# SyncE's row reads in a five-layer graph network: byte offsets from lists, 32 registers a load, h_edge zeroed in quarters

## The chip, the core and the metric

The kernel runs on one core of a Trainium2 chip. The metric is the device time of one execution in microseconds; lower is better. The time before is the median of three runs.

## The reference

Five graph layers run one after the other on 12,500 nodes and 412,500 edges sorted by destination node, with 64 features a node. Each of the first four reads, for every edge, one row of a table of transformed source nodes, and adds the weighted rows up for each destination:

```python
def _rgat_conv(x, src, dst, etype, W, Q, K, b):          # layers 0 and 1 (CONV1, CONV2); 8 relations, 4 heads
    xw = jnp.einsum('ni,rio->rno', x, W)
    alpha = jax.nn.leaky_relu(qn[etype, dst] + kn[etype, src], 0.2)
    ex = jnp.exp(alpha - amax[dst])
    attn = ex / (denom[dst] + 1e-16)
    out_j = xw[etype, src].reshape(-1, H, hc // H)
    agg = jax.ops.segment_sum(attn[:, :, None] * out_j, dst, num_segments=n)
```

Layer 2 (GAT) is the same with one relation and one head; layer 3 (RGCN) sums `xw[etype, src] * edge_weight`; layer 4 (GINE) adds a message relu(h[src] + edge_attr) from every edge and runs a small network of two matrix products on the sum. What matters here is the read `xw[etype, src]` or `h[src]`: 412,672 rows (with padding) of 256 to 272 bytes in each of four layers.

## The kernel before, in words

Edges lie in 128 partitions of 3,224 edges each. A layer's edge pass goes over them in 52 chunks of 62 columns (`CH = 52`, `J = 62`), so a chunk is 128 x 62 edges. The loop body holds two chunks, `b` = 0 and 1, with a buffer `G[:, b]` each, and runs 26 times. I call two chunks a pair, and the edge pass of layer l pass l.

A chunk's rows come from two engines at once. GpSimd (POOL) issues one indirect DMA for each of the first 61 columns (`JP = J - 1`), each of 128 rows, through the helper `gather` (L652, called in the loop of L767 to L771). SyncE (SP) reads the last column, row by row. For each chunk it loads a list of 128 row numbers from DRAM into `row_list` (L607), waits until the buffer may be written (`idx_ready`, L609) and until the list is in (`list_in`, L611), loads 16 numbers at a time into registers (`sp.load`, L613, `RUN = 16`), copies them (`snap`, L614) and issues one small DMA for each row (L615): 128 DMAs a chunk. In pass 0 alone it also writes a 2 MB slice of zeros into `h_edge` after every chunk (L619), which layer 4 needs and GpSimd waits for at L721 (`big_zero`).

VectorE (DVE) waits for both sources of a chunk (`gathered` and `rows_in`, L1946 to L1948; in RGCN L1849 to L1851), then does the scores and the running sums (L1950 onwards) with ScalarE (ACT). In the middle of that work it copies the indices of the chunk two further on (`next_indices`, L1911) and raises `idx_ready`, which lets GpSimd and SyncE refill that buffer. ScalarE stores the sums (L870 to L879). When the last chunk's sums are stored, GpSimd reads the sums at the ends of the nodes (`gather_ends`, L652 with `fix_i` and then `end_i`), and the next layer's table is made.

Ahead of pass 0 lies a start of some 447 us. In it SyncE issues the input loads in order, among them two that pick one column out of every chunk (L522, L523: `src` and `edge_type_8` as `c p j` with j fixed, so that every element of 4 bytes stands alone), then the two stores of `dst_f` and `sub_last` (L528, L529). These two stores release GpSimd's first indirect reads, the search for the ends of the nodes, whose results the rest of the start needs. VectorE makes the relation-specific row numbers from the two lists at L1329, and SyncE writes both lists to DRAM (L531, L532).

## Time and profile before

| What | Value |
|---|---|
| Median device time of 3 runs | 36401.83 us (36386.37 to 36415.52) |
| Span of the profiled execution, first to last instruction | 22678.7 us |
| What the trace does not cover (median less span) | 13723.1 us |
| PE busy | 5315.0 us, 23% |
| DVE busy | 10606.0 us, 47% |
| ACT busy | 5421.1 us, 24% |
| POOL busy | 16413.3 us, 72% |
| POOL `region<-table,idx` (L652) | 12688 indirect DMAs, 944 ns each |
| SP `region<-table` (L615) | 26624 DMAs |

The page gives no total time for the profiled execution beside its span; the 13723.1 us between the span and the median are seen in no view. Engines work in parallel, so busy shares don't add up; a "releaser" is what ended an engine's idle time. SP's own instructions (register loads, register arithmetic, DMA issues) are not counted as busy, but they are listed with their durations as SPq.

### The profile page before, as it was taken

How to read it: one execution, taken by the hardware profiler on the slowest of the kernel's cores; microseconds unless marked ns; L12 is line 12 of the kernel's file. 1: busy time of each engine (PE TensorE's matmuls, PEld its weight loads, DVE VectorE, ACT ScalarE, POOL GpSimd, SP SyncE). 2: the span in 40 equal slices, each digit the busy share in tenths (PEclk: the TensorE clock that was granted, in tenths of full speed). 3: DMA queues.
4: the chain of work that ended last, by engine and by line, in shares of the span. 5: the costliest groups of instructions: out<-in, count | busy, mean ns of one | idle time of the engine just before them, and what ended most of it. 6: DMA issues, size and time to landing. Idle time of an engine off the chain costs nothing.

```text
span 22678.7 us, 201879 instructions
## 1 busy us (share of the span) xinstructions
PE 5315.0 (23%) x30665; PEld 3876.7 (17%) x30665; DVE 10606.0 (47%) x9480; ACT 5421.1 (24%) x4707; POOL 16413.3 (72%) x17069
## 2 busy tenths in 40 slices
PE   2000000020000001222222266666662222222201
PEld 1000000010000001222222255555552000000001
DVE  2444444324444443556566668888884111111167
ACT  1222222222222222111111132222221211121175
POOL 7777777677777776777777767777776777777733
PEclk9999999999999999666666655555555666666655
DMA  6333333332222222222222232222222222222164
GB/s 203 95 98 101 95 98 98 88 97 76 70 75 70 72 73 46 54 54 58 54 57 55 52 87 56 52 56 52 56 52 61 84 76 76 76 80 80 66 235 162
DMA packets 782414, 1839.84 MB, mean 81 GB/s; under 512 B 380834, under 2 KB 415306, under 8 KB 720302
## 3 DMA queue, kind: packets, MB, share of 16 engines
q0 software_dynamic: 544128, 569.36, 13.8%
q10 hardware_dynamic: 88736, 721.35, 8.1%
q1 hardware_dynamic: 148622, 541.43, 6.7%
q14 instruction: 915, 7.50, 0.1%
q8 instruction: 13, 0.21, 0.0%
HBM read 1007.43 MB, written 929.12 MB: 85 GB/s over the span
## 4 chain that ended last, share of the span: by engine, by line
POOL 55%; issue 24%; SPq 12%; DMA 3%; DVE 2%; PE 2%; ACT 1%; POOLq 0%; DVEq 0%; ACTq 0%
POOL region L652 41%; POOL by_src L742 12%; SPq L615 9%; SPq L613 3%; DMA region<-by_src 2%; DMA row_list<-row_lists 1%; POOL q_rel L713 1%; SPq L614 1%; PE ps L1207 1%; DVE region L1567 1%; DVE region L1538 0%; PE ps L1168 0%; POOL h_edge L725 0%; PE ps L1209 0%; POOL q_one L713 0%
## 5 line engine op out<-in xcount | busy, mean ns | idle before, releaser
L652 POOL DMA_INDIRECT region<-table,idx x12688 | 11972.1, 944 | 3941.9 <-issue 3873.2
L742 POOL DMA_INDIRECT by_src<-region,idx x3224 | 3122.7, 969 | 1007.9 <-issue 1001.5
L1950 DVE TENSOR_TENSOR region<-ps,region 128x248 f32<-128x248 f32 (+1 forms) x156 | 74.4, 477 | 3958.0 <-DMA region<-table,idx 1967.5
L1216 PE MATMUL ps<-ident,region 128*68 128x128 f32 (+1 forms) x3 | 1.3, 444 | 8044.9 <-DVE region L2013 8044.9
L1767 DVE TENSOR_TENSOR region<-ps,region 128x2048 bf16<-128x2048 f32 x833 | 1845.8, 2216 | 18.2 <-DVE region L1761 8.0
L870 ACT COPY region<-region 128x4216 f32<-128x4216 f32 (+1 forms) x156 | 1182.2, 7579 | 2477.7 <-DVE region L1996 2477.7
L1112 PE MATMUL ps<-region 98*128 98x128 f32 x6448 | 1657.9, 438 | 323.3 <-DVEq L1833 192.8
L1533 DVE CAST region<-src 128x62 f32 (+1 forms) x52 | 11.7, 224 | 3463.8 <-DMA by_src<-region,idx 3463.6
L1207 PE MATMUL ps<-region,ident 128*128 128x512 f32 (+1 forms) x832 | 809.5, 1062 | 3141.2 <-DVE region L1538 3141.2
L1112 PEld LDWEIGHTS ps<-region 98*128 98x128 f32 x6448 | 1455.9, 330 | 410.7 <-DVEq L1833 269.7
L1905 DVE TENSOR_TENSOR_SCAN region<-region,ps 128x1008 f32<-128x1008 f32 x624 | 1382.9, 2244 | 10.7
L1216 PEld LDWEIGHTS ps<-ident,region 128*68 128x68 f32 (+1 forms) x3 | 0.4, 150 | 8045.6 <-DVE region L2013 8045.6
L1902 DVE TENSOR_TENSOR ps<-region,ps 128x1008 f32<-128x1008 f32 x624 | 1192.1, 1940 | 105.2 <-ACT ps L906 96.2
L1916 DVE TENSOR_TENSOR_SCAN region<-region,ps 128x2016 f32<-128x2016 f32 x104 | 452.8, 4354 | 1582.6 <-ACT region L900 1582.6
L905 ACT ACTIVATE region<-ps 128x248 f32<-128x248 f32 (+1 forms) x156 | 50.5, 324 | 4560.1 <-DVE ps L1964 4560.1
L944 ACT COPY region<-ps 98x512 f32<-98x512 f32 x832 | 476.3, 572 | 2703.7 <-PE ps L1095 2702.0
L1065 PE MATMUL ps<-later,ident_b 128*128 128x512 bf16 x832 | 376.6, 453 | 2884.7 <-DVE region L1809 2884.7
L980 ACT COPY ps<-region 128x1008 f32<-128x1008 f32 x208 | 381.8, 1852 | 2143.0 <-DVE region L1538 2143.0
L1105 PE MATMUL ps<-region 128*98 128x128 bf16 x3224 | 540.5, 320 | 1150.6 <-DVE region L1819 1150.5
L1207 PEld LDWEIGHTS ps<-region,ident 128*128 128x128 f32 x832 | 175.9, 219 | 3376.2 <-issue 3376.2
L903 ACT ACTIVATE region<-ps 128x4032 f32<-128x4032 f32 x52 | 183.6, 3532 | 2235.6 <-DVE ps L1964 2235.6
L1819 DVE TENSOR_TENSOR region<-region,ps 98x512 f32<-98x512 f32 x832 | 552.2, 664 | 185.9 <-PE ps L1112 185.9
(291 smaller groups left out, 16216.1 us busy)
## 6 DMA issues: line engine op xcount, KB each, us to landing
sums<-region ACTq DMA_DIRECT2D x104, 2232.0 KB
region<-table SPq DMA_DIRECT2D x13312, 0.3 KB
sums<-region ACTq DMA_DIRECT2D x104, 1984.0 KB, 11.1
region<-table,idx POOLq DMA_INDIRECT x12688
region<-table SPq DMA_DIRECT2D x6656, 0.3 KB
region<-table SPq DMA_DIRECT2D x6656, 0.2 KB
sums<-region ACTq DMA_DIRECT2D x52, 2046.0 KB
region<-by_src SPq DMA_DIRECT2D x52, 2015.0 KB, 9.6
```

The lines of the kernel that those rows point to most:

```text
L613: sp.load(indices, row_list[0:1, b, p0:p0 + RUN])
L615: sp.dma_start(G[p0 + k:p0 + k + 1, b, J, :], tables[l][bass.ds(row, 1), :]).then_inc(rows_in[l][b][2 * p0 // P], 16)
L652: pool.indirect_dma_start(out=to, out_offset=None, in_=table, in_offset=bass.IndirectOffsetOnAxis(ap=index, axis=0)).then_inc(s, 16)
L742: pool.indirect_dma_start(out=by_src, out_offset=bass.IndirectOffsetOnAxis(ap=idx[:, b, j:j + 1], axis=0), in_=MSG[:, b, j, :], in_offset= ...
L870: last = act.copy(O[:, :, 0:D + h], OT[:, 0:D + h, 1:J1].rearrange("p f j -> p j f"))
L1105: pe.matmul(ps[0:HI, 1, (j % QUAD) * LO:(j % QUAD + 1) * LO], HOT[RGCN][:, m % 2, j % GROUP, 0, 0:HI], HOT[RGCN][:, m % 2, j % GROUP, 1, : ...
L1112: last = pe.matmul(ps[:, 6 + n % 2, c * LO:(c + 1) * LO], AT[0:HI, n % 2, c * LO:(c + 1) * LO], BASE[0:HI, c, :], start=True, stop=True)
L1207: pe.matmul(o, ident[:, :], XS[:, :, 1 + j0:1 + j1].rearrange("p f j -> p j f"), start=True, stop=False)
L1767: tt(HOT[l][:, m % 2, 0:n], it, bc(HALF[l][1][b][:, js[0]:js[0] + n, :], 3, LO), ALU.is_equal).then_inc(ab_ready, 1)
L1819: tt(flat[0:HI, 0:w], flat[0:HI, 0:w], ps[0:HI, 1, 0:w], ALU.add).then_inc(h_add, 1)
L1902: return tt(wg[q % 2].rearrange("p (f j) -> p f j", f=PF), rows, bc(weight[q], 1, PF), ALU.mult)
L1905: return dve.tensor_tensor_scan(OT[:, piece(q), :].rearrange("p f j -> p (f j)"), REP[:, piece(q), :].rearrange("p f j -> p (f j)"), wg[q ...
```

## The change

1. The lists hold byte offsets instead of row numbers. VectorE multiplies the row numbers by the row's size in bytes once, at the start, and makes three lists (for CONV1 and CONV2, GAT, RGCN). The DMA of a row then addresses the table and the buffer as bytes.
2. The lists have room for two columns (`ROWS = 256`), and the start loads both columns, with four strided loads instead of two. Still only the last column is read row by row (`ROWED = 1`; k runs from 128 to 255), and GpSimd keeps 61 columns.
3. 32 registers are filled by one load (`RUN = 32`), so that a chunk has 4 loads instead of 8.
4. The lists of both chunks of a pair are requested at the start of the pair, each with a semaphore of its own, instead of each just ahead of its chunk.
5. `h_edge` is zeroed in quarters: pass l writes quarter l after each chunk (0.5 MB), in all four passes.
6. ScalarE waits for the table's stores before a pass; the `rows_in` semaphores are shared by the passes, and VectorE clears them ahead of passes 1 to 3.

```diff
-JP = J - 1
-RUN = 16
+ROWED = 1
+RUN = 32
+ROWS = 2 * P
+ROW_GROUPS = [(P, P + 64), (P + 64, ROWS)]
+ROW_KIND = {0: 0, 1: 0, 2: 1, 3: 2}
+QUARTERS = 4
...
+        def row_place(l, b, k):
+            j, p = divmod(k, P)
+            return slots(l)[1][p:p + 1, b, J - 1 + j, :].bitcast(U8)
+
+        def row_bytes(l, at):
+            n = 4 * row_in(l)
+            return tables[l].bitcast(U8).rearrange("n f -> (n f)")[bass.ds(at, n)].unsqueeze(0)
...
-            sp.dma_start(row_list[:, 1, :], a["src"].rearrange("(p c j) -> c p j", p=P, c=CH)[:, :, J - 1]).then_inc(loaded, 16)
-            sp.dma_start(row_list[:, 0, :],
-                         a["edge_type_8"].rearrange("(p c j) -> c p j", p=P, c=CH)[:, :, J - 1]).then_inc(loaded, 16)
+            for j in range(2):
+                of = slice(j * P, (j + 1) * P)
+                sp.dma_start(list_src[:, of],
+                             a["src"].rearrange("(p c j) -> c p j", p=P, c=CH)[:, :, J - 2 + j]).then_inc(loaded, 16)
+                sp.dma_start(list_type[:, of],
+                             a["edge_type_8"].rearrange("(p c j) -> c p j", p=P, c=CH)[:, :, J - 2 + j]).then_inc(loaded, 16)
...
+                mine = (P, ROWS)
                 with sp.Fori(0, CH // 2) as i:
                     for b in range(2):
-                        sp.dma_start(row_list[0:1, b, :], row_lists[bass.ds(i * 2 + (kind + b), 1), :]).then_inc(list_in, 16)
+                        sp.dma_start(row_list[b:b + 1, mine[0]:mine[1]],
+                                     row_lists[bass.ds(i * 2 + (CH * ROW_KIND[l] + b), 1),
+                                               mine[0]:mine[1]]).then_inc(list_in[b], 16)
+                    for b in range(2):
                         sp.wait_ge(idx_ready, i * 2 + ((CH + 2) * l + b + 1))
                         sp.sem_inc(chunk_begun, 1)
-                        sp.wait_ge(list_in, i * 32 + 16 * (CH * l + b + 3))
+                        sp.wait_ge(list_in[b], i * 16 + 16 * (CH // 2 * l + 1))
                         sp.sem_inc(chunk_begun, 1)
-                        for p0 in range(0, P, RUN):
-                            sp.load(indices, row_list[0:1, b, p0:p0 + RUN])
-                            for k, row in enumerate([sp.snap(r) for r in indices]):
-                                sp.dma_start(G[p0 + k:p0 + k + 1, b, J, :],
-                                             tables[l][bass.ds(row, 1), :]).then_inc(rows_in[l][b][2 * p0 // P], 16)
-                        if l == CONV1:
-                            he = h_edge.rearrange("(p j) k -> p (j k)", p=P)
-                            sp.dma_start(he[:, bass.ds(i * (2 * J * D) + b * J * D, J * D)], zeros_d).then_inc(big_zero, 16)
+                        for k0 in range(mine[0], mine[1], RUN):
+                            n = min(RUN, mine[1] - k0)
+                            sp.load(indices[0:n], row_list[b:b + 1, k0:k0 + n])
+                            for k, row in enumerate([sp.snap(r) for r in indices[0:n]]):
+                                sp.dma_start(row_place(l, b, k0 + k),
+                                             row_bytes(l, row)).then_inc(rows_in[b][row_group(k0 + k)], 16)
+                        he = h_edge.rearrange("(p j) k -> p (j k)", p=P)
+                        w = J * D // QUARTERS
+                        sp.dma_start(he[:, bass.ds(i * (2 * J * D) + (b * J * D + l * w), w)], zeros_d[:, 0:w]).then_inc(big_zero, 16)
...
-                    pool.wait_ge(big_zero, 16 * CH)
+                    pool.wait_ge(big_zero, 16 * CH * QUARTERS)
...
+                if l in SUMMED:
+                    for q in range(GP):
+                        act.wait_ge(stored[q], 16 * TURNS * (l + 1))
...
-            dve.wait_ge(loaded, 16 * 7)
-            stt(out=row_list[:, 0, :], in0=row_list[:, 1, :], scalar=float(REL), in1=row_list[:, 0, :], op0=ALU.mult,
-                op1=ALU.add).then_inc(lists_ready, 1)
+            dve.wait_ge(loaded, 16 * 9)
+            done(stt(out=list_type, in0=list_src, scalar=float(REL), in1=list_type, op0=ALU.mult, op1=ALU.add))
+            settle()
+            done(ts_(row_list[:, :], list_type, 4.0 * row_in(CONV1), None, ALU.mult))
+            done(ts_(list_src, list_src, 4.0 * row_in(GAT), None, ALU.mult))
+            settle()
+            ts_(list_type, list_type, 4.0 * row_in(RGCN), None, ALU.mult).then_inc(lists_ready, 1)
...
+                if l:
+                    for b in range(2):
+                        for part in range(len(ROW_GROUPS)):
+                            dve.sem_clear(rows_in[b][part])
```

## Rows read from the trace of the kernel before

**Rows 1.** Windows: us, then each engine's busy time (PE, PEld, DVE, ACT, POOL), clock, DMA, GB/s

```profile
447.00:4500.00 4053.00, 4.22 (x18) 3.68 (x18) 1651.69 (x1369) 959.33 (x388) 2993.06 (x3172) 1.00 0.35 96
13300.00:17200.00 3900.00, 2429.39 (x12752) 2165.34 (x12750) 3200.18 (x2828) 1042.88 (x1231) 2947.44 (x3125) 0.50 0.21 54
```

**Rows 2.** Chain that ended last, shares by line, window of pass 0, then of pass 1

```profile
by line: SPq L615 48.4%; issue 25.3%; SPq L613 14.6%; DMA row_list<-row_lists 6.5%; SPq L614 3.7%; SPq L619 0.8%; ACT region L870 0.2%; DVE region L1905 0.2%; DVE ps L1902 0.1%; SPq L605 0.1%; SPq L607 0.1%; DMA region<-table 0.0%; SPq L611
...
by line: POOL region L652 75.0%; issue 24.9%; POOLq L766 0.1%; POOLq L769 0.0%; POOLq L768 0.0%
```

**Rows 3.** Timeline of POOL: start us, us, op, idle before; passes 0 and 1

```profile
447.18 0.96 POOL L652 DMA_INDIRECT region<-table,idx  x1 [2.95 <-issue]
...
4509.73 0.94 POOL L652 DMA_INDIRECT region<-sums,fix_i  x1 [98.03 <-DMA sums<-region]
...
4778.93 0.97 POOL L652 DMA_INDIRECT region<-table,idx  x1 [2.97 <-issue]
...
8777.22 0.94 POOL L652 DMA_INDIRECT region<-sums,fix_i  x1 [38.46 <-DMA sums<-region]
```

**Rows 4.** Groups of POOL, window of pass 0: count, busy us, mean ns, idle before

```profile
L652 POOL DMA_INDIRECT region<-table,idx x3172 | 2993.1, 944 | 974.4 <-issue 966.5 <-DVE idx L1911 7.9
```

**Rows 5.** Timeline of SP, one pair of pass 0: start us, us, line, count

```profile
1375.12 0.23 SPq L607 DMA_DIRECT2D row_list<-row_lists  x1
1379.56 67.04 SPq L615 DMA_DIRECT2D region<-table  x128
1446.78 0.58 SPq L619 DMA_DIRECT2D h_edge<-zeros_d  x1
1447.56 0.27 SPq L607 DMA_DIRECT2D row_list<-row_lists  x1
1457.01 67.06 SPq L615 DMA_DIRECT2D region<-table  x128
...
1530.00 0.23 SPq L607 DMA_DIRECT2D row_list<-row_lists  x1
```

**Rows 6.** Waits of SP: us in total, times, longest; windows of passes 0, 1 and 3

```profile
SPq L611 <- DMA row_list<-row_lists: 237.7, 52, 7.3
...
SPq L609 <- DVE idx L1911: 104.9, 26, 5.7
...
SPq L609 <- DVE idx L1858: 189.1, 42, 6.3
```

**Rows 7.** SP lines L613 to L615, window of pass 0: ns min/median/max

```profile
L613 SPq TENSOR_LOAD <-row_list x416: 1138/1229/3980, 450.8 to 4463.5; - x139
...
L614 SPq FUSED_REGOPS  x832: 166/180/191, 452.0 to 4465.0; - x167
...
L615 SPq MOVE region<-table x6656: 29/29/37, 452.9 to 4471.6; - x196
L615 SPq DMA_DIRECT2D region<-table x6656: 212/213/1072, 452.9 to 4471.6; - x196
L615 SPq FUSED_REGOPS  x6240: 37/37/48, 453.3 to 4471.5; - x195
```

**Rows 8.** Timeline of SP at the start: start us, us, line

```profile
23.62 2.77 SPq L522 DMA_DIRECT2D row_list<-in_src  x1
26.43 4.31 SPq L523 DMA_DIRECT2D row_list<-in_edge_type  x1
30.79 4.26 SPq L528 DMA_DIRECT2D dst_f<-region  x1
```

**Rows 9.** DMA packets, window 26.5 to 35.5 us

```profile
DMA packets 13908, 0.09 MB, mean 10 GB/s; under 512 B 13908, under 2 KB 13908, under 8 KB 13908
```

**Rows 10.** Timeline of POOL and of DVE at the start

```profile
41.22 3.31 POOL L652 DMA_INDIRECT region<-sub_last,region  x1 [35.36 <-DMA sub_last<-region]
...
48.58 3.15 POOL L652 DMA_INDIRECT region<-sub_last,region  x1 [0.30 <-issue]
...
47.41 3.50 DVE L1319 SCALAR_TENSOR_TENSOR region<-cont,region 128x3223 f32<-128x3223 f32 x1
```

More of the change, by code:

```diff
@@ L10 @@
 BF16 = mybir.dt.bfloat16
+U8 = mybir.dt.uint8
 ACT = mybir.ActivationFunctionType
@@ L166, in build @@
         edge0 = sb("edge0", [P, 1])
[L167 removed]
+        row_list = sb("row_list", [CH, ROWS], I32)
         iota_r = sb("iota_r", [P, REL])
@@ L332, in build @@
         lists_ready = sem("lists_ready")
-        list_in = sem("list_in")
-        rows_in = {l: [[sem(f"rows_in{l}_{b}_{k}") for k in range(2)] for b in range(2)] for l in SUMMED}
+        lists_out = sem("lists_out")
+        list_in = [sem(f"list_in{b}") for b in range(2)]
+        rows_in = [[sem(f"rows_in{b}_{k}") for k in range(len(ROW_GROUPS))] for b in range(2)]
         dst_ready = sem("dst_ready")
@@ L502, in piece, with gathered_columns, row_group @@
             return slice(q * PF, (q + 1) * PF)
+        lists = wide[0:CH].rearrange("p a b -> p (a b)").bitcast(I32)
+        list_src, list_type = lists[:, 0:ROWS], lists[:, ROWS:2 * ROWS]
+        def row_place(l, b, k):
[4 more added lines that the diff above has]
+            return tables[l].bitcast(U8).rearrange("n f -> (n f)")[bass.ds(at, n)].unsqueeze(0)
+        def gathered_columns(l):
+            return J - ROWED
+        def row_group(k):
+            return [lo <= k < hi for lo, hi in ROW_GROUPS].index(True)
         block = ctx.enter_context(nc.Block())
@@ L530, in _ @@
             sp.wait_ge(lists_ready, 1)
-            sp.dma_start(row_lists[0:CH, :], row_list[:, 0, :]).then_inc(list_in, 16)
-            sp.dma_start(row_lists[CH:2 * CH, :], row_list[:, 1, :]).then_inc(list_in, 16)
+            sp.dma_start(row_lists[0:CH, :], row_list[:, :]).then_inc(lists_out, 16)
+            sp.dma_start(row_lists[CH:2 * CH, :], list_src).then_inc(lists_out, 16)
+            sp.dma_start(row_lists[2 * CH:3 * CH, :], list_type).then_inc(lists_out, 16)
             for l in LAYERS:
@@ L598, in _ @@
                     sp.dma_start(q_to, q_rows[:, 0:w]).then_inc(e_in, 16)
-                kind = 0 if REL_OF[l] > 1 else CH
                 for q in range(GP):
@@ L769, in _ @@
                         pool.sem_inc(chunk_begun, 1)
-                        for j in range(JP):
+                        for j in range(gathered_columns(l)):
                             gather(G[:, b, 1 + j, :], tables[l], idx[:, b, j:j + 1], gathered[l][b])
@@ L1848, in piece_step @@
                             if q == 0:
-                                dve.wait_ge(gathered[l][b], i * (16 * JP) + 16 * JP)
-                                for half in range(2):
-                                    dve.wait_ge(rows_in[l][b][half], i * (8 * P) + 8 * P)
+                                dve.wait_ge(gathered[l][b], i * (16 * gathered_columns(l)) + 16 * gathered_columns(l))
+                                for part, (lo, hi) in enumerate(ROW_GROUPS):
+                                    dve.wait_ge(rows_in[b][part], i * (16 * (hi - lo)) + 16 * (hi - lo))
                             elif not ranks:
@@ L1945, in _ @@
                                 dve.tensor_copy(first_f[:, ob, :], src1[:, bass.ds(at + J, J)]).then_inc(hl_ready, 1)
-                            dve.wait_ge(gathered[l][b], i * (16 * JP) + 16 * JP)
-                            for half in range(2):
-                                dve.wait_ge(rows_in[l][b][half], i * (8 * P) + 8 * P)
+                            dve.wait_ge(gathered[l][b], i * (16 * gathered_columns(l)) + 16 * gathered_columns(l))
+                            for part, (lo, hi) in enumerate(ROW_GROUPS):
+                                dve.wait_ge(rows_in[b][part], i * (16 * (hi - lo)) + 16 * (hi - lo))
                             done(tt(Qs, qv, G[:, b, 1:J1, D:ri].rearrange("p j h -> p h j"), ALU.add))
```

7 lines of the change are left out of this document (2 added, 5 removed).

## The prediction

> **What bounds the kernel now.** I read the windows by stage first, then the chain of waits of single passes, then POOL's timeline at the ends of passes, then SP's own instructions. In a pass POOL is busy about three quarters of the time: 2993.06 us of 4053 in pass 0 and 2947.44 of 3900 in pass 3, while DVE has 1651.69 and 3200.18 [rows 1]. POOL's remaining quarter is no real idleness: of 974.4 us before its reads in pass 0, 966.5 are "issue", 0.305 us before each of 3172, and only 7.9 us are a wait for indices [rows 4]. So a read costs POOL 0.944 + 0.305 = 1.249 us, a pair of chunks 2 x 61 x 1.249 = 152.4 us, and a pass 26 x 152.4 = 3962 us.
>
> The chain of waits then shows that the four passes are not alike [rows 2]. In pass 1 the chain is POOL's L652 and its issue time, nothing else. In pass 0 it is SP: its row DMAs (L615), register loads (L613), the copies (L614), and 6.5% for the row list coming in. The price of that is read at the ends of the passes [rows 3]. POOL's first read of the ends (`fix_i`) needs the last sums. In pass 1 it comes 38.46 us after POOL's last row read, which is the last chunk's unavoidable work; in pass 0 it comes after 98.03 us. From the first row read to that point pass 0 takes 4509.73 - 447.18 = 4062.55 us, pass 1 takes 8777.22 - 4778.93 = 3998.29 us. Both have the same 3172 reads and the same kind of chunk, so pass 0 loses 64.3 us to SP and no more.
>
> SP's pair in pass 0 lasts 1530.00 - 1375.12 = 154.9 us [rows 5], 2.5 us more than POOL's 152.4; 26 times that is 65 us, the same loss by a second way. In passes 1 and 3 SP waits for DVE's indices, 104.9 us and 189.1 us in all [rows 6]: there it is ahead, if not by much, and making it quicker gives nothing.
>
> **The change part by part.**
>
> *SP's work in a pair.* From the first row DMA to the last a chunk takes 67.04 us [rows 5], with 7 loads inside. A load is 1.229 us and its two copies 2 x 0.180 [rows 7], together 1.59 us. So a row costs (67.04 - 7 x 1.59) / 128 = 0.437 us, its gaps included; of this the DMA, MOVE and FUSED_REGOPS that the trace lists are 0.213 + 0.029 + 0.037 [rows 7]. That FUSED_REGOPS works out the address; with a byte offset there is still a base to be added, so I cost the row the same. A gain there of at most 0.037 + its gap is possible, and a loss is a rival below.
>
> A load of 32 registers isn't in the trace. Bounds: as dear as one of 16 (1.59 us with two copies) or twice that (3.18 us). Then a chunk's rows with all four loads take 128 x 0.437 + 4 x 1.59 = 62.3 us or 55.9 + 4 x 3.18 = 68.7 us; before it was 67.04 + 1.59 = 68.6. I take 65.5, the middle, since the row shows neither end to be nearer.
>
> The rest of a pair is 154.9 - 2 x 68.6 = 17.7 us. Of it 237.7 / 26 = 9.1 us are waits for the list [rows 6]. In the pair shown, the second list is requested 0.8 us after a 2 MB write of zeros began, and its chunk's rows start 9.4 us after the request [rows 5]; the first one takes 4.4 us, load included. The new order requests both lists ahead of the first chunk, so the second wait, about 7 us (the longest is 7.3), goes. The rest is 10.7 us, with one more short issue for the zeros in passes 1 to 3 (0.58 us a chunk).
>
> Sum: 2 x 62.3 + 10.7 = 135 us to 2 x 68.7 + 10.7 = 148 us, middle 142. All are below 152.4. In pass 0 POOL becomes the last to finish, as in pass 1, and SP's slack is 4 to 17 us a pair. So the gain is capped at the 64.3 us of above, however quick SP gets, and the three means (32 registers, lists ahead, quarter zeros) overlap: each that saves over 2.5 us a pair would do it alone. What is late next is POOL's 1.249 us a read, which the change leaves alone.
>
> The Trainium skill, "Runtime: NRT & Kernel Launch", section "Instruction fetch mechanics", speaks against this part: it says that a register load costs about 200 ns for each register even in bulk. The trace doesn't agree, since by that rule 16 registers would take 3.2 us where the row shows 1.229 us. By the rule applied to 32 registers a load would be 6.4 us and a pair some 2 x (55.9 + 4 x 7.1) + 10.7 = 179 us, an estimate from that page; the sum above doesn't use it.
>
> *Zeros in all passes.* Each pass gets 26 MB more (pass 0: 77 MB less of its 103). DMA is busy to 0.35 in pass 0 and 0.21 in pass 3 [rows 1]; pass 0 holds the full amount and POOL's reads there cost 944 ns and only 7.9 us of waiting [rows 4]. So the moved writes are covered by POOL's pace, cost 0, and if that cover were gone, up to the 0.58 us issue for each of 52 chunks, 30 us a pass. The last zeros are issued after SP's last rows of pass 3, well ahead of layer 4's wait for them.
>
> *The start.* Here the change costs. The strided loads L522 and L523 stand ahead of the stores L528 and L529 in SP's order, and POOL's first read at 41.22 us waits for the latter [rows 10]. Two more of them are added. Their issues took 2.77 + 4.31 = 7.1 us [rows 8]; the packets behind them, 2 x 52 x 128 = 13312 of 4 bytes, go at 13908 in 9 us [rows 9], so 8.6 us for as many again. POOL's chain then runs through the start to pass 0, so a shift of its beginning reaches pass 0 in full. But not all of it is lost: POOL's reads at 41.22 and 48.58 last 3.31 and 3.15 us where others last 0.94, the second beside a long DVE instruction that ends at 47.41 + 3.50 [rows 10]. Started 8.6 us later, POOL meets one of the two, and saves 2.3 us. Bounds 0 and 9; I take +6. DVE's added instructions on the lists (four of 52 x 256, where the trace has one of half that size, of 0.28 us) lie beside POOL's reads; at most 1 us, within the bounds.
>
> *Waits and clears.* ACT's new wait is for the stores for which POOL and SP wait anyhow before the pass; behind it on ACT stands the first chunk's copy, which is needed only once rows have come. DVE's four clears before passes 1 to 3 are semaphore instructions; nothing to 1 us each. I take 0.
>
> **The sum.** -64.3 + 6 = -58 us, from -75 to -45 with the bounds of the start and of the tails. On the span: 22678.7 - 58 = 22621 us. The median of the runs shown is 13723 us above the span, in something that no view shows; I carry it over unchanged: 36401.8 - 58 = 36344 us, that is -0.16%. About 0.2%, 73 us, is what a measurement of this kernel can tell from no change, so the likeliest verdict is "same", though the mechanism gains.
>
> **The rivals.**
> 1. *SP stays last in pass 0.* If 32 registers cost as 32 times one and the first list wait grows by what the second loses, SP's pair stays at 155 us; only the start's cost is left: 36408 us. Against it: 2.5 us a pair is enough, and the zeros' part in the list wait shrinks too. 0.08.
> 2. *SP becomes the bound in all passes, slower.* The place is L615. If the byte address takes one more register instruction for each row, at 0.037 us plus as much again for its gap, a pair grows by 256 x 0.073 = 19 us to 161, 8.4 over POOL's. Over 104 pairs that is 874 us, less the 64 that pass 0 loses already, plus 6: about 37220 us. It decides from (152.4 - 142) / 256 = 0.04 us a row. For it: the margin is thin against a row of 0.437 us. Against it: the row number needed a multiplication, the offset doesn't. 0.05.
> 3. *The load grows faster than its registers.* By the longest load seen, 3.98 us [rows 7], and four copies: 2 x (55.9 + 4 x 4.70) + 10.7 = 160 us, 7.7 over, so some 36401.8 + 104 x 7.7 - 58 = 37140 us. The price in the skill's page "Runtime: NRT & Kernel Launch" is of this kind. 0.03, as the one row on loads speaks against it.
> 4. *What lies outside the span moves.* 1% of 13723 us is 137 us: 36207 or 36481 us. Nothing says that it depends on the kernel's instructions. 0.08, of which 0.06 are below.
>
> **How the numbers follow.** My forecast has 0.76, own range 36320 to 36365; in 0.12 of it the gain and the scatter of the runs (29 us between three) together pass 73 us. Faster by over 0.2%: 0.12 + 0.06 = 0.18. Within: 0.64 + 0.08 = 0.72. Slower: 0.05 + 0.03 + 0.02 = 0.10. The range takes in rival 1 and the scatter: 36290 to 36410; outside are rivals 2 to 4 (0.16) and a rest of 0.03.
>
> **What the profile after would show.** Right: POOL's wait before the `fix_i` read of pass 0 falls from 98 to about 38 us; the chain in pass 0 is L652 and issue, as in pass 1; SP waits for indices (L609) in pass 0 too; SP's pair work is 135 to 148 us; POOL's first read starts at 47 to 50 us instead of 41.22, and pass 0 begins near 453. Wrong: SP on the chain of any pass, a row that takes over 0.48 us, a load over 5 us, or a median that moves where the span doesn't.

## The result, and the profile after

The changed kernel takes 33804.58 us (median of 4 runs, 33766.30 to 33810.79), the kernel before 36395.41 us (4 runs, 36386.37 to 36415.52). The ratio is 0.9284, with a 95% interval of 0.9271 to 0.9298: 7.2% faster, 2591 us. The prediction said 36344 us, no measurable change.

The first thing to compare in the two profiles is the span with the time of the same run. The profiled run of after took 33766.3 us and its span is 33764.6 us, 1.7 us less. The trace of before had a span of 22678.7 us beside runs of 36402 us. So the kernel before was profiled once more, unchanged (e1_before). The tops of its page and of the page of after:

```profile
span 36273.4 us, 201879 instructions
```

```profile
span 33764.6 us, 176251 instructions
...
## 4 chain that ended last, share of the span: by engine, by line
issue 29%; another core or an unknown queue 28%; SPq 24%; DVE 10%; PE 5%; ACT 1%; DMA 1%; POOL 1%; ACTq 0%; DVEq 0%; POOLq 0%
```

The new trace of before belongs to a run of 36275.1 us, so 1.7 us lie outside it as well. The trace that the prediction rests on shows an execution unlike any later one of the same program: each of the runs below has a span within 2 us of its time. The record has neither a total time for that execution nor a span for the three runs it was set beside, and what made it so short is open. The comparison is therefore made between after and e1_before. Their windows of the four passes (us, busy time of PE, PEld, DVE, ACT and POOL, granted clock, DMA share, GB/s), after first:

```profile
546.00:6766.00 6220.00, 3.58 (x16) 3.49 (x16) 1598.25 (x1315) 931.61 (x377) 2992.93 (x3172) 1.00 0.19 49
7245.00:13486.00 6241.00, 0.21 (x1) 0.13 (x1) 1599.42 (x1312) 899.57 (x352) 2992.57 (x3172) 1.00 0.19 49
13939.00:20316.00 6377.00, 1264.74 (x13081) 1012.32 (x13283) 2336.11 (x2247) 623.24 (x377) 2992.53 (x3172) 0.57 0.16 38
20715.00:27755.00 7040.00, 2430.06 (x12686) 2156.99 (x12686) 3176.19 (x2820) 1033.69 (x1222) 2992.63 (x3172) 0.50 0.13 34
```

```profile
540.00:7690.00 7150.00, 3.58 (x16) 3.48 (x16) 1597.94 (x1315) 931.72 (x377) 2993.96 (x3172) 1.00 0.19 54
8196.00:15105.00 6909.00, 0.46 (x2) 0.37 (x2) 1599.00 (x1312) 899.63 (x352) 2992.32 (x3172) 1.00 0.16 41
15579.00:22604.00 7025.00, 1340.73 (x13282) 1028.75 (x13283) 2341.44 (x2247) 623.24 (x377) 2992.90 (x3172) 0.57 0.13 31
23033.00:30245.00 7212.00, 2430.03 (x12686) 2156.43 (x12686) 3174.82 (x2815) 1035.31 (x1222) 2992.05 (x3172) 0.50 0.11 29
```

Each engine's busy time in a pass is the same in both within 1%, but for PE's in pass 2 (1264.74 and 1340.73 us, with 201 matmul records fewer after), and POOL's is that of the old trace too (2993.06 us [rows 1]). Only the length of a pass differs: 4053 us in the old trace, 7150 in e1_before, 6220 after. In the executions that were timed, POOL is busy for less than half of a pass and does not bound it. The granted clock is the same before and after, pass by pass, and has no part in the result.

In e1_before SP is last in all four passes; after, in passes 0 and 1 alone. The chains of waits by line: e1_before in a stretch of pass 3, then after in stretches of passes 0 and 2 ("another core or an unknown queue" is time whose releaser the profile can't name):

```profile
by line: SPq L615 49.5%; issue 40.2%; SPq L613 6.5%; SPq L614 2.7%; DMA row_list<-row_lists 0.8%; SPq L607 0.1%; SPq L605 0.1%; SPq L611 0.0%; SPq L609 0.0%; SPq L608 0.0%; SPq L610 0.0%
...
by line: SPq L645 49.2%; issue 40.6%; SPq L643 6.1%; SPq L644 3.1%; SPq L649 0.5%; SPq L633 0.2%; SPq L631 0.1%; SPq L639 0.0%; SPq L637 0.0%; SPq L638 0.0%; SPq L640 0.0%
...
by line: another core or an unknown queue 50.8%; issue 13.5%; DVE region L1808 9.3%; DVE ps L1943 6.2%; DVE region L1946 5.4%; DVE region L1850 5.0%; ACT region L899 2.1%; PE ps L1098 1.2%; SPq L645 1.1%; PE ps L1102 1.1%; PE ps L1103 1.0%;
```

And SP's timeline (start us, us, line), two chunks of before in e1_before, then two of after; the answers to [rows 5]:

```profile
2018.66 129.48 SPq L615 DMA_DIRECT2D region<-table  x128
2148.33 0.58 SPq L619 DMA_DIRECT2D h_edge<-zeros_d  x1
...
2157.43 129.35 SPq L615 DMA_DIRECT2D region<-table  x128
```

```profile
2080.53 113.36 SPq L645 DMA_DIRECT2D region<-table  x128
2194.08 0.58 SPq L649 DMA_DIRECT2D h_edge<-zeros_d  x1
2197.88 113.49 SPq L645 DMA_DIRECT2D region<-table  x128
```

128 rows took 67.04 us in the old trace; the same instructions take 129.48 us here and 113.36 us after the change. The chunk's rows are long because SP runs at two speeds. Its line L645 in a stretch of 60 us within that chunk, beside the three instructions of a row of before in its slow stretch (ns min/median/max; first and last start):

```profile
L645 SPq MOVE region<-table x21: 689/700/1397, 2105.2 to 2164.1; - x21
L645 SPq DMA_DIRECT2D region<-table x20: 13/699/710, 2105.9 to 2162.7; - x20
```

```profile
L615 SPq MOVE region<-table x12: 15/700/702, 2050.5 to 2097.4; - x12
L615 SPq DMA_DIRECT2D region<-table x12: 13/700/701, 2051.2 to 2098.8; - x12
L615 SPq FUSED_REGOPS  x10: 4/700/709, 2051.9 to 2096.0; - x10
```

A MOVE takes 700 ns here where [rows 7] has 29, and it is the same for every kind. The 41 instructions in (2164.1 - 2105.2) = 58.9 us are one per 1.4 us. There is no FUSED_REGOPS at L645 any more. POOL's timeline shows when SP is slow:

```profile
2088.97 0.94 POOL L682 DMA_INDIRECT region<-table,idx  x1 [42.51 <-DVE idx L1952]
...
2163.89 0.94 POOL L682 DMA_INDIRECT region<-table,idx  x1 [0.30 <-issue]
...
2212.42 0.94 POOL L682 DMA_INDIRECT region<-table,idx  x1 [47.59 <-DVE idx L1952]
```

POOL's 61 reads of the chunk run without a break from 2088.97 to 2164.8 us. SP's slow stretch is from 2101.5 to 2171 us: it begins 12 us after the first read and ends 6 us after the last. The last chunk of pass 0 is the check within the same execution. POOL's last read starts at 6765.32 us, and SP's 128 rows behind it take 53.20 us instead of 113:

```profile
6799.72 53.20 SPq L645 DMA_DIRECT2D region<-table  x128
```

The length of a chunk's rows can then be worked out. In 70 us at 1.4 us each SP gets through 50 instructions: that is 25 rows of two, or under 17 rows of three. The other rows go at 0.31 us after and 0.40 us before (the median distance of two rows in the run e7_one_column below and in the old trace; 0.35 and 0.42 on average). From the first row to the last a chunk holds three loads of 32, each with four copies (2.12 + 3 x 0.18 + 0.04 = 2.7 us), or seven of 16 with two copies (1.59). So after has 70 + 103 x 0.31 + 8 = 110 us (113.36 in the trace), and before 70 + 111 x 0.40 + 11 = 125 us (129.48). This was worked out behind the result; the runs below test it.

In the table: us per chunk, from POOL's first to its last read of a pass by 52, for the kernels of this document.

| kernel | time us | before, same chip | pass 0 | 1 | 2 | 3 |
|---|---|---|---|---|---|---|
| before, old trace | 36401.8 | | 76.2 | 76.2 | 76.2 | 76.2 |
| e1_before | 36275.1 | 36254.1 | 137.5 | 132.9 | 135.1 | 138.7 |
| after | 33804.6 | 36395.4 | 119.6 | 120.0 | 122.6 | 135.4 |
| e2_row_numbers | 35711.9 | 36254.1 | 132.2 | 132.0 | 134.2 | 135.9 |
| e3_run16 | 33822.2 | 36254.1 | 120.3 | 120.4 | 122.8 | 135.7 |
| e4_no_rows | 29729.6 | 36254.1 | 86.4 | 86.3 | 119.7 | 132.0 |
| e5_after | 33591.0 | 36268.7 | 119.0 | 119.1 | 122.4 | 134.1 |
| e6_act_extra | 33609.3 | 36268.7 | 119.1 | 119.2 | 122.5 | 134.5 |
| e7_one_column | 20461.7 | 36268.7 | 58.1 | 58.7 | 57.3 | 67.0 |
| e8_offsets_alone | 33956.5 | 36268.7 | 124.0 | 119.3 | 122.5 | 135.6 |
| e9_zeros_first | 33753.2 | 36424.7 | 120.7 | 118.3 | 122.6 | 135.8 |
| e10_16_rows | 34039.8 | 36424.7 | 121.8 | 122.2 | 122.5 | 135.8 |
| e11_no_rows | 29836.5 | 36424.7 | 86.6 | 86.4 | 120.3 | 132.2 |
| e12_lists_late | 33898.3 | 36424.7 | 120.6 | 120.6 | 123.4 | 135.8 |
| e13_pauses | 27449.2 | 36247.7 | 89.5 | 90.1 | 102.3 | 99.4 |
| e14_no_rows_pauses | 25917.2 | 36247.7 | 86.4 | 86.3 | 90.7 | 90.1 |
| e15_before_pauses | 28812.1 | 36247.3 | 94.8 | 93.1 | 107.6 | 109.4 |
| e16_no_rows_pauses | 25939.2 | 36247.3 | 86.4 | 86.3 | 90.8 | 90.1 |

The runs were made on several chips, and before was timed on each: 36247 to 36425 us. So times are to be compared by their ratio to it.

### The profile page after: what moved, and what is told of

It reads as the page before. It is cut to its first block, busy times and chain, and to the rows that moved or that the text cites. A ratio compares the mean times of both kernels' runs of the same rounds, so it can differ in the third digit from the quotient of the medians.

```text
span 33764.6 us, 176251 instructions
## 1 busy us (share of the span) xinstructions
PE 5826.4 (17%) x30457; PEld 4128.6 (12%) x30665; DVE 10608.5 (31%) x9483; ACT 5430.4 (16%) x4707; POOL 16518.7 (49%) x17069
## 3 DMA queue, kind: packets, MB, share of 16 engines
q0 software_dynamic: 544128, 569.36, 8.7%
## 4 chain that ended last, share of the span: by engine, by line
issue 29%; another core or an unknown queue 28%; SPq 24%; DVE 10%; PE 5%; ACT 1%; DMA 1%; POOL 1%; ACTq 0%; DVEq 0%; POOLq 0%
SPq L645 19%; DVE region L1808 3%; SPq L643 2%; PE ps L1145 2%; DVE region L1871 1%; DVE ps L1943 1%; SPq L644 1%; DVE region L1946 1%; DVE region L1850 1%; DMA region<-by_src 1%; DVE region L1860 1%; PE ps L1201 1%; PE ps L1138 1%; ACT region L899 1%
## 5 line engine op out<-in xcount | busy, mean ns | idle before, releaser
L772 POOL DMA_INDIRECT by_src<-region,idx x3224 | 3271.6, 1015 | 1245.9 <-issue 1051.0
L1575 DVE TENSOR_TENSOR_SCAN region<-region,ps 128x1008 f32<-128x1008 f32 x208 | 451.7, 2234 | 3243.4 <-ACT ps L1013 2993.6
L1946 DVE TENSOR_TENSOR_SCAN region<-region,ps 128x1008 f32<-128x1008 f32 x624 | 1382.8, 2244 | 10.7
L1850 DVE TENSOR_TENSOR region<-ps,region 128x1024 bf16<-128x1024 f32 (+1 forms) x416 | 493.4, 1186 | 1302.6 <-remote 1085.3
L1138 PEld LDWEIGHTS ps<-region 128*98 128x98 bf16 x3224 | 365.5, 191 | 3848.9 <-DVE region L1860 3364.4
L1102 PE MATMUL ps<-ident_b,region 128*128 128x128 bf16 x3224 | 613.2, 266 | 1280.4 <-issue 1066.0
```

The costliest lines, as they stand in the source:

```text
L772: pool.indirect_dma_start(out=by_src, out_offset=bass.IndirectOffsetOnAxis(ap=idx[:, b, j:j + 1], axis=0), in_=MSG[:, b, j, :], in_offset= ...
L1138: pe.matmul(ps[0:HI, 1, (j % QUAD) * LO:(j % QUAD + 1) * LO], HOT[RGCN][:, m % 2, j % GROUP, 0, 0:HI], HOT[RGCN][:, m % 2, j % GROUP, 1, : ...
L1850: tt(same_b[:, m % 2, 0:n, :], ps[:, 6:8, :].rearrange("p a (c i) -> p (a c) i", i=P)[:, 0:n, :], bc(first_f[:, b, js[0]:js[0] + n], 2, P) ...
L1946: return dve.tensor_tensor_scan(OT[:, piece(q), :].rearrange("p f j -> p (f j)"), REP[:, piece(q), :].rearrange("p f j -> p (f j)"), wg[q ...
```

## The experiments

**The kernel before, once more, and the parts of the change.** e1_before is before.py as it stands.

> The kernel before, unchanged, for a trace that belongs to a run of about 36,400 us; the trace shown before covers only 22,679 us. Theory A: SyncE is the bound of all four passes, since its instructions become slow (about 0.7 to 1.4 us each, as in the trace of the changed kernel) while GpSimd streams its indirect reads. Then the span here is about 36,390 us, a chunk takes some 12 us more than in the changed kernel (120 us in pass 0, so about 132), and the slow instructions of SyncE are seen here too. Rival B: the time outside the trace is spent before or after the work and the passes take 76 us a chunk as in the first trace; then the span is 22,680 us and the passes last 3,960 us each.

It gave the 36273.4 us span and SP's 129.48 us of above, as theory A has it, with 137.5 us a chunk in pass 0 where 132 had been expected. Against it after gains 17.9, 12.9, 12.5 and 3.3 us a chunk in the four passes, 46.6 x 52 = 2423 of the 2509 us between the spans.

e2_row_numbers is after with the rows addressed by number again. The lists are multiplied by 1.0, and:

```
-            n = 4 * row_in(l)
-            return tables[l].bitcast(U8).rearrange("n f -> (n f)")[bass.ds(at, n)].unsqueeze(0)
+            return tables[l][bass.ds(at, 1), :]
```

> The changed kernel with row numbers instead of byte offsets, so that every row DMA again needs an address instruction (FUSED_REGOPS) of its own: 3 instructions a row instead of 2. Theory A1 (the number of SyncE instructions is what counts, each slow one costing the same): 128 more of about 286 a chunk; with about half of a chunk's 120 us slow, it gives most of the 12 us a chunk back: 35,500 to 36,400 us. Theory A2 (the row DMAs or the loads are what is slow, not the instruction count): 33,900 us, within 0.5% of the changed kernel.

35711.94 us, 0.985 of before, where after has 0.926 to 0.929. The FUSED_REGOPS is back at each row, and SP's chunk in pass 0 reads

```profile
2117.64 125.12 SPq L644 DMA_DIRECT2D region<-table  x128
```

12 us over after's 113.36. By the table the offsets bring 12.6, 12.0, 11.6 and 0.5 us a chunk: 36.7 x 52 = 1908 us, 76% of the 2509 (by the ratios to before, 79% of the gain). Theory A1 holds.

e3_run16 has `RUN = 16`, all else as after.

> The changed kernel with 16 registers a load instead of 32: 8 loads a chunk instead of 4. A 32-register load took 2.12 us in the changed kernel's trace, a 16-register load 1.23 in the first one, so alone it costs 4 x (2 x 1.23 - 2.12) = 1.4 us a chunk, 0.28 ms over 208 chunks: 34,080 us. If the loads are what made the gain (rival to A1), 35,500 us or more.

33822.24 us, 0.9329, against 0.9262 and 0.9284 of after. In the passes it is 0.7, 0.4, 0.2 and 0.3 us a chunk over the first profile of after, and 1.3, 1.3, 0.4 and 1.6 over e5_after's. 34,080 us had been expected, so the longer load brings less than its cost alone promised. SP's loads of 32 registers in pass 0 of after

```profile
L643 SPq TENSOR_LOAD <-row_list x202: 668/2119/2141, 549.9 to 6692.2; - x101
```

take 2.12 us where those of 16 took 1.229 [rows 7], which is 56 ns for each further register; with their copies four of 32 are 10.8 us a chunk and eight of 16 are 12.7. The Trainium skill, "Runtime: NRT & Kernel Launch", section "Instruction fetch mechanics", has about 200 ns for each register; this trace doesn't agree.

e8_offsets_alone takes from the change the offsets alone: RUN is 16, each list is requested ahead of its own chunk, and all zeros are written in pass 0.

> Byte offsets (and the room for two columns in the lists) alone: 16 registers a load, each list requested just ahead of its chunk, all zeros in pass 0. The row numbers gave 35,712 against 36,254 of the kernel before and about 33,800 of the changed one, so the offsets should be worth about 1,900 us by themselves and the rest about 550: 34,350 us here. If the parts only help together, 35,000 or more.

33956.49 us, 0.9362. From 1 to 0.9362 is 86% of the way to e5_after's 0.9262 on the same chip. The 34,350 us expected took the parts as adding up; they overlap, since the offsets bring 86% when they stand alone and 76 to 79% when they are taken away. In passes 1 and 2 it equals e5_after within 0.3 us a chunk; in pass 0 it stays 5.0 us a chunk behind e5_after.

e9_zeros_first is after with the zeros as before, e12_lists_late with the list's request inside the chunk's loop:

```
-                        w = J * D // QUARTERS
-                        sp.dma_start(he[:, bass.ds(i * (2 * J * D) + (b * J * D + l * w), w)], zeros_d[:, 0:w])...
+                        if l == CONV1:
+                            sp.dma_start(he[:, bass.ds(i * (2 * J * D) + b * J * D, J * D)], zeros_d)...
```

```
                     for b in range(2):
                         sp.dma_start(row_list[b:b + 1, ...
-                    for b in range(2):
                         sp.wait_ge(idx_ready, ...
```

> The changed kernel with all of h_edge zeroed in pass 0, 2 MB after each chunk, as in the kernel before. In the run with the offsets alone pass 0 took 124 us a chunk where pass 1 took 119 with the same instructions. If the 2 MB of zeros make that difference: 4.9 us x 52 = 250 us more, 33,840 us; if it was the list's late request that made it, under 50 us more.

> The changed kernel with each chunk's list requested just ahead of the chunk again. In the trace of the kernel before SyncE waits 312.7 us in all for its lists, 3 us a pair in the passes without zeros; the new order has 22.4 us of that. So 200 to 400 us more than the changed kernel, 33,800 to 34,000 us, all of it in passes 0 to 2; nothing in pass 3, where VectorE's indices come last.

e9 has 0.9267 and e12 0.9306. Within e9's own trace the pass with the zeros costs 120.7 us a chunk and the next one 118.3: writing them all in one pass costs 2.4 us a chunk there, half of the 4.9 that it was asked about, and what passes 1 to 3 save by not having any gives about as much back (pass 1: 118.3 against 120.0 of after). Lists late cost 0.6 to 1.0 us a chunk. After, SP waits 22.4 us in the whole run for its lists, and in e1_before 312.7 us:

```profile
SPq L640 <- DMA row_list<-row_lists: 22.4, 52, 2.7
```

```profile
SPq L611 <- DMA row_list<-row_lists: 312.7, 203, 6.6
```

These 290 us are at most half of the 601 us that the offsets leave of the gain; how the rest divides among loads, lists and zeros, the single runs don't tell. Single runs of the same kernel lie 0.2% apart (0.9262 and 0.9284 for after), so the order of e9, e12 and e3 among themselves isn't settled.

**Is SP the bound, and of which passes?** e4_no_rows has `ROWED = 0`: POOL reads all 62 columns and SP no row at all. e11_no_rows is the same kernel, timed four times.

> The changed kernel with the last column given back to GpSimd: 62 indirect reads a chunk, SyncE reads no row and loads no list in the passes (it still writes the zeros). The output is the full one. Theory A: without SyncE's rows the passes go at GpSimd's pace, 52 x 62 x 1.249 = 4,026 us each instead of 6,220 to 7,040, so about 24,000 us. Rival C: the stream of indirect reads slows every engine by itself, with or without SyncE; then the passes keep most of their length and it is over 28,000 us.

> The changed kernel with the last column read by GpSimd too, timed against the kernel before: it took 29,730 us where the kernel before took 36,254. The theory (SyncE's rows bound passes 0 and 1, GpSimd's stream with VectorE and TensorE behind it bounds 2 and 3) says 0.82 of the kernel before, 0.88 of the changed one; the output is the full one.

29729.6 us and 29836.5 us; the ratio of e11 is 0.8193 (0.818 to 0.8207). It beats after by 12%. The time is what rival C had expected, over 28,000 us; theory A's 24,000 is far off. In passes 0 and 1 POOL, now alone on the chain, goes at 86.4 us a chunk. So rows by SP cost 33 us a chunk more than reading the column by POOL, in the kernel whose split was meant to relieve POOL. The 86.4 us are still 9 over 62 x 1.249 = 77.4: POOL's own reads take 1058 ns on average there instead of 944, and 41% of those of pass 0 start over 1.3 us after the one before, many of them in this pace of 1.40 us:

```profile
2067.97 1.09 POOL L677 DMA_INDIRECT region<-table,idx  x1 [0.30 <-issue]
2069.37 1.09 POOL L677 DMA_INDIRECT region<-table,idx  x1 [0.30 <-issue]
```

Passes 2 and 3 gain only 3 us: there SP isn't the bound after the change. Their length has to do with PE and DVE. After's timeline in pass 3:

```profile
24175.75 0.69 DVE L1860 TENSOR_TENSOR region<-region,ps 98x512 f32<-98x512 f32 x1 [28.36 <-issue]
...
24176.49 0.66 PE L1138 MATMUL ps<-region 128*98 128x128 bf16 x4 [29.11 <-DVE region L1860]
```

DVE stands for 28.36 us at an instruction of 0.69 us with nothing that it waits for ("issue"), and PE behind it for 29.11. Stretches of 28 to 44 us of this kind are in passes 2 and 3, 87 to 90% of DVE's time in them inside POOL's streams of reads.

**What makes the others slow?** e5_after is after once more, e7_one_column lets POOL read one column of the 61 (the other 60 aren't read, so that part of the input of each sum is left out).

> The changed kernel, unchanged, as the base of this set on the same chip: 33,600 to 33,850 us by either theory.

> The changed kernel with GpSimd reading 1 column of a chunk instead of 61 (the other 60 columns of the buffer keep what they held, so their part of the computation is left out); SyncE reads its 128 rows as before. Theory A: without the stream of indirect reads no instruction of SyncE is slow, a row takes 0.31 us, a chunk's rows with their loads about 50 us instead of 113, and the passes go at the pace of VectorE and ScalarE, 50 to 75 us a chunk: 19,500 to 23,000 us in all. Rival E (128 small DMAs in a row fill SyncE's own queue, and it is slow by itself): its rows still take over 100 us a chunk and the time is over 30,000 us.

e5_after took 33590.98 us, 0.9262 of before. e7's SP, the same kind of chunk and the same instructions of L645:

```profile
1515.07 53.09 SPq L645 DMA_DIRECT2D region<-table  x128
...
L645 SPq MOVE region<-table x26624: 29/29/39, 554.6 to 14506.4; - x199
L645 SPq DMA_DIRECT2D region<-table x26624: 217/224/1054, 554.7 to 14506.4; - x199
```

Not one of 26624 MOVEs takes over 39 ns. So SP's slowness comes with POOL's reads, and without it 128 rows take 53 us, as in the last chunk of after. The whole kernel falls to 20461.65 us, as theory A has it.

e6_act_extra asks whether the engines share a budget of instructions, so that more instructions on ACT cost SP time:

```
+                        for n in range(24):
+                            act.copy(extra[:, n:n + 1], bias[:, 0:1])
```

> The changed kernel with 24 copies of one element a partition added on ScalarE in every chunk of passes 0 to 2, where ScalarE waits for VectorE's scores and GpSimd's indirect reads run. Theory A (while those reads run, the instructions of all engines together go at one in about 0.70 us, so that every instruction of an idle engine takes a place): up to 24 x 0.70 = 17 us more a chunk, 156 chunks, so 34,300 to 36,400 us. Rival D (only SyncE's own instructions are slow, by its share of the DMA path): ScalarE idles there for tens of us, the copies take under 0.2 us each, and the time stays within 0.3% of the changed kernel.

33609.28 us, 18 us over e5_after on the same chip, and the time is the rival's. Only about five of a chunk's 24 copies fall into the slow stretch (in pass 0 252 of 1224 wait, 261.3 us in all), so a shared budget would by them have cost some 5 x 0.70 x 156 = 550 us and not the expected 700 to 2800. The 18 us are far below that too, and SP's 128 rows take 113.62 us, as without the copies: no shared budget shows. Yet ACT isn't free either. ACT's copies are slow in the same stretch:

```profile
2104.77 0.19 ACT L936 COPY extra<-bias 128x1 f32<-128x1 f32 x1 [1.21 <-issue]
2106.18 0.19 ACT L936 COPY extra<-bias 128x1 f32<-128x1 f32 x1 [1.22 <-issue]
2107.58 0.19 ACT L936 COPY extra<-bias 128x1 f32<-128x1 f32 x1 [1.21 <-issue]
```

One starts each 1.40 us, SP's own pace. In this run ACT and SP each have that pace for themselves while POOL streams.

e10_16_rows keeps POOL's instructions and makes each read 16 rows instead of 128 (the rows of the other 112 partitions aren't read):

```
-                            gather(G[:, b, 1 + j, :], tables[l], idx[:, b, j:j + 1], gathered[l][b])
+                            gather(G[0:16, b, 1 + j, :], tables[l], idx[0:16, b, j:j + 1], gathered[l][b])
```

> The changed kernel with 16 rows in each of GpSimd's 61 indirect reads instead of 128 (the other 112 partitions of those columns keep what they held, so their part of the computation is left out). With one indirect read a chunk SyncE was never slow and the kernel took 20,462 us. If the number of rows moved (packets) makes SyncE slow, this one is near that, 20,500 to 24,000 us, the passes at GpSimd's pace of 76 us a chunk at most. If it is the stream of GpSimd's instructions, whatever they move, SyncE's instructions stay at 1.4 us each while it runs, and the time stays above 31,000 us.

34039.79 us, 0.9345, above the 31,000 us that stood for the stream of instructions. POOL's queue moves a third of the bytes (193 MB for 569), and nothing gets quicker:

```profile
q0 software_dynamic: 544128, 192.78, 2.7%
...
L682 POOL DMA_INDIRECT region<-table,idx x3058 | 2567.1, 839 | 3584.2 <-DVE idx L1953 2666.9 <-issue 917.2
```

```profile
2109.52 115.59 SPq L645 DMA_DIRECT2D region<-table  x128
```

The packets are as many as with 128 rows, 544128, and a read still takes POOL 839 ns. So it isn't the data; it may be the packets, the instructions or their records, which this run leaves alike.

**Is it the stream's length?** Since SP goes slow only 12 us after the stream's start, short bursts should leave it alone. e13_pauses is after, with a wait for landing after each 10 reads:

```
                         for j in range(gathered_columns(l)):
                             gather(G[:, b, 1 + j, :], tables[l], idx[:, b, j:j + 1], gathered[l][b])
+                            if (j + 1) % 10 == 0:
+                                pool.wait_ge(gathered[l][b], i * (16 * gathered_columns(l)) + 16 * (j + 1))
+                                pool.sem_inc(chunk_begun, 1)
```

> The changed kernel with GpSimd waiting, after every 10 of its 61 indirect reads, until these have landed (about 6 us each time, so its stream of 76 us becomes one of 105 to 115 us in bursts of 12.5 us). The slow stretch began some 12 us after the stream did. Theory F (something fills up during an unbroken stream): SyncE's instructions stay quick, its rows take about 55 us a chunk, GpSimd's 105 to 115 us become the bound, passes 0 to 2 shrink by 5 to 10%: 32,000 to 33,200 us. Theory G (each indirect read makes SyncE slow for as long as it is under way): SyncE is slow for the longer stream, 1.4 us each: 135 us or more a chunk, over 35,500 us.

27449.21 us, 0.757 of before and 18% under after, by six waits added to each chunk. The direction is theory F's, the size is not: 32,000 us or more was expected, with 6 us for each wait and with passes 0 to 2 shorter alone. POOL's timeline at a pause, and SP's chunks beside it:

```profile
1615.24 0.95 POOL L682 DMA_INDIRECT region<-table,idx  x1 [0.30 <-issue]
...
1618.62 0.94 POOL L682 DMA_INDIRECT region<-table,idx  x1 [2.43 <-DMA region<-table,idx]
```

```profile
1551.85 61.15 SPq L645 DMA_DIRECT2D region<-table  x128
...
1640.96 61.29 SPq L645 DMA_DIRECT2D region<-table  x128
```

A pause costs POOL 2.43 us instead of 0.30, so 12.8 us a chunk, and the rows fall from 113.36 to 61.15 us. A wait for landing also keeps no more than ten reads under way and makes the reads fewer per us. Which of the three, the break, the number under way or the rate, is what helps was not tried apart. Now the chain of pass 0 is what the prediction had expected of after:

```profile
by line: POOL region L682 59.7%; issue 32.6%; DMA region<-table,idx 7.5%; POOLq L804 0.1%; POOLq L796 0.0%; POOLq L799 0.0%; POOLq L798 0.0%
```

e15_before_pauses puts the same waits into the kernel before, to see what the change is worth when the stream's effect is gone.

> The kernel before with the waits of e13_pauses after every 10 of GpSimd's reads, nothing else. If the change gains only where SyncE's instructions are stalled, the two are then alike: GpSimd's chunk of 89 us is above SyncE's 77, so about 27,500 us here, within 300 us of the changed kernel with pauses. If byte offsets and the rest gain by themselves, since SyncE's chunk is its own bound even with pauses, 100 us or more a chunk in passes 0 to 2: over 29,000 us.

28812.12 us, 0.795 of before: neither expectation holds. It is 1363 us, 5%, above e13. Its rows still take 84 to 89 us a chunk, and SP remains on its chain:

```profile
by line: SPq L615 48.3%; issue 37.0%; SPq L613 9.1%; SPq L614 2.9%; DMA row_list<-row_lists 1.5%; SPq L619 0.6%; SPq L607 0.3%; SPq L610 0.2%; SPq L605 0.1%; SPq L609 0.0%; SPq L608 0.0%; SPq L611 0.0%
```

By e13's rows plus what before has more (128 x 0.09 us for the FUSED_REGOPS, and 7 x 1.59 - 3 x 2.7 = 3 us for the loads) 76 us would do. The 9 to 13 us above that aren't explained; part of SP's slow stretch seems to stay where SP is the later of the two.

**The version that beats both.** e14_no_rows_pauses is e4's kernel with the pauses in passes 2 and 3 alone, where PE and DVE stand still; e16_no_rows_pauses is the same, timed four times.

```
+                            if l in (GAT, RGCN) and (j + 1) % 10 == 0:
+                                pool.wait_ge(gathered[l][b], ...)
+                                pool.sem_inc(chunk_begun, 1)
```

> The kernel without SyncE's rows (29,836 us) with the same waits after every 10 reads, in passes 2 and 3 alone, where a chunk takes 120 and 132 us though GpSimd streams for only 78 of them and VectorE and TensorE then stand still for 28 to 44 us at a time. Theory F: they no longer stand still, VectorE's 45 and 61 us a chunk lie beside the reads, and a chunk takes GpSimd's 107 to 115 us: 28,300 to 29,100 us. Theory G: they stall as before and the stream is longer, over 31,500 us.

> The fastest kernel so far, timed against the kernel before: no rows by SyncE, GpSimd pauses after every 10 reads in passes 2 and 3. One look gave 25,917 against 36,248 us, so 0.715; the output is the full one.

25917.18 us and 25939.24 us; the ratio to before is 0.7155 (0.7143 to 0.7167). Passes 2 and 3 fall from 119.7 and 132.0 us a chunk (e4) to 90.7 and 90.1, near POOL's own pace with its pauses (77.4 + 12.8 = 90.2). The 28,300 us expected for this theory had counted 6 us for a wait here too. Windows of pass 3, e4 first, then e14:

```profile
16892.00:23754.00 6862.00, 2433.62 (x12702) 2159.91 (x12702) 3185.08 (x2821) 1032.67 (x1223) 3048.70 (x3224) 0.50 0.13 34
```

```profile
15317.00:20002.00 4685.00, 2468.11 (x12898) 2193.03 (x12898) 3246.83 (x2867) 1050.84 (x1244) 3041.50 (x3224) 0.50 0.19 51
```

The busy times are the same within 2%, and 2177 us of standing still are gone.

## Why the prediction was wrong, point by point

**The span against the median: the step that failed first.** The prediction noted 13723 us between the span and the runs, said that no view shows them, and carried them over unchanged. They were inside the passes: e1_before has 137.5, 132.9, 135.1 and 138.7 us a chunk where the old trace has 76.2, which is 239.4 x 52 = 12449 of the 13595 us between the two spans. The views of [rows 1 to 6] are right for an execution of a kind that no run with a span on record was. The mismatch was the largest number in sight and should have been the first rival, with a price: spread over the 26624 rows of SP, 0.515 us a row, over 0.437 a row by the trace. Rival 4 named the place but gave it 1% and no mechanism.

**POOL as the bound, and the cap of 64.3 us.** Wrong for the timed runs. The cap was POOL's 152.4 us a pair; the real pairs took 266 to 277 us with SP last in all four passes, so nothing capped the gain at 64.3 us, and "making it quicker gives nothing" fell with that. Only in pass 3 is it nearly so: the whole change brings 3.3 us a chunk there and the offsets 0.5, because the stand-stills of PE and DVE come last as soon as SP is a little quicker.

**The price of a row.** "I cost the row the same", for an addition that might remain. It doesn't remain: L645 is a MOVE and a DMA. The possible gain was put at 0.037 us and its gap; outside the stream it is 0.40 - 0.31 = 0.09 us, and within it, one full slot of 1.4 us. This term alone is the 1908 us of e2. Rival 2 had the right place (one register instruction a row, at L615, counted once for each of 256 rows a pair) and the wrong sign.

**The load of 32 registers.** The bounds were 1.59 and 3.18 us with its copies, and 2.12 + 3 x 0.18 + 0.04 = 2.7 lies between them, nearer the upper one; the middle, 2.4, was taken. Rival 3 is out.

**List waits and zeros.** SP's waits for the lists went, as said (22.4 us in all are left). Their size was small only beside the cap: with SP last they count, 0.6 to 1.0 us a chunk by e12. The moved zeros were put at nothing for passes 1 to 3, covered by POOL; with SP last they cost pass 1 1.7 us a chunk (120.0 against 118.3 of e9), where pass 0 gains 1.1 (119.6 against 120.7).

**The start.** Right: POOL's first read was said to move from 41.22 to 47 to 50 us. In e1_before it begins at 43.15 us, after at 50.27; pass 0 begins at 540.47 and 546.25 us, 5.8 us later for the 6 predicted. That sum was made from the old trace's start, which is 93 us shorter, so part of its closeness may be luck.

```profile
50.27 1.42 POOL L682 DMA_INDIRECT region<-sub_last,region  x1 [44.41 <-DMA sub_last<-region]
...
546.25 0.96 POOL L682 DMA_INDIRECT region<-table,idx  x1 [3.04 <-issue]
...
6890.82 0.94 POOL L682 DMA_INDIRECT region<-sums,fix_i  x1 [124.56 <-DMA sums<-region]
```

**The signs that were named.** POOL's wait before the `fix_i` read of pass 0 was to be 38 us; it is 124.56, because SP's last row ends at 6852.9 us, long after POOL's last read, and 38 us pass behind that row. SP waits for no indices in pass 0, and its pair takes 240.9 us (2080.53 to 2321.45) and not 135 to 148. Of the signs of being wrong, SP is on the chain of passes 0 and 1, and a row takes 113.36 / 128 = 0.89 us, over 0.48. "A median that moves where the span doesn't" was the wrong question: against e1_before both moved together.

## What to carry to other kernels

Compare a trace's span with the time of the runs before reading anything else, and if they differ by more than the 2 us that no later trace here reaches, take another trace or price the difference as a mechanism of the kernel. On an engine that only issues, count instructions and not their durations: where each costs a slot, one register instruction fewer for each row was worth three quarters of a 7% gain. And when one engine streams indirect DMAs, look at what the other engines' short instructions take meanwhile; a few waits in the stream (18% here) may be worth more than moving work away from it.

## What the runs showed of the hardware that was not expected

In the stretches followed here, while POOL issues indirect reads without a break (one each 1.25 us), SP slows down after about 12 us to one instruction each 1.40 us whatever its kind (29 ns becomes 700 in the record), until about 6 us after the stream. ACT has the same pace in e6, in passes 2 and 3 PE and DVE have stand-stills of 28 to 44 us, and where POOL streams through a whole pass (e4) its own reads lengthen from 944 to 1058 ns. It doesn't depend on the bytes read (e10), nor, as far as five copies a chunk can tell, on what ACT issues beside SP (e6); SP's part is absent with one read a chunk (e7), and with bursts of 10 most of it is gone (e13 to e16), less so in e15.

What in the chip does it isn't shown. A rival that stands is that recording the instructions takes part in it. No run settles that: every run of after and of the experiments has a span beside its time, so all were recorded, and none shows what the kernels take without it. The gains of the pauses are those of such runs. The Trainium skill, "NOTIFIC — the notification-queue block", section "7.1 Overflow: three behaviours, one of which stalls the engine", says that the block's own pipeline holds its producers up and never loses a record; that would fit a common pace for all kinds of instructions, and no run here shows it. Nor was it tried whether the number of packets or that of POOL's instructions matters. And why one execution of before went at 76.2 us a chunk, with POOL streaming and no MOVE of SP in pass 0 over 37 ns [rows 7], is open; it shows that the stream alone isn't enough.
